# Decoder layer on one core: the four output-weight splits of a head group placed one by one in the order of VectorE and ScalarE

## The reference, cut to what matters

```
x = layernorm(x + attention(x))            # 4 x 512 tokens, width 512
x = layernorm(x + scan_block(ctx, z=x))    # a state-space scan, 16 states
x = layernorm(x + experts(x))              # shared and 16 routed experts

# attention, differential: 8 heads in 4 groups g, each with two maps
p = softmax(q1 k1) - lam * softmax(q2 k2)  # causal
o = p v;  o = o * rsqrt(mean(o*o) + eps) * subln_w * (1 - lambda_init)
return o.reshape(B, S, 2048) @ out_w.T + out_b

# scan, in 512 channels and 16 states
state = state * exp(dt * A) + (dt * u) * b;  y = sum over states of state * c
```

## Time and profile before

| | us |
|---|---|
| median of 3 runs (lowest, highest) | 1616.1 (1615.11, 1616.11) |
| the profiled execution | 1615.29 |
| its span, first to last instruction | 1613.4 |
| busy: TensorE, VectorE, GpSimd, ScalarE | 1397.1, 1294.5, 1137.9, 1045.1 |
| mean granted TensorE clock | 0.933 of full speed |

### The profile page before, as it was taken

One profiled execution on the slowest core, in us unless ns is written; L12 is line 12 of the kernel. 1 busy time (PEld: TensorE's weight loads), 2 busy tenths in 40 slices (PEclk: granted clock), 3 DMA queues, 4 the chain that ended last, 5 costly groups with the idle time before them and its releaser, 6 DMA issues.

```text
span 1613.4 us, 23141 instructions
## 1 busy us (share of the span) xinstructions
PE 1397.1 (87%) x7536; PEld 1139.5 (71%) x7536; DVE 1294.5 (80%) x2377; ACT 1045.1 (65%) x2411; POOL 1137.9 (71%) x613
## 2 busy tenths in 40 slices
PE   3655789999999989899989899986579998998996
PEld 1213678877888978788878788874367676776784
DVE  4898688998888998888989899898548577486575
ACT  3888466766666767667657666664458567577474
POOL 1335489888889987789988799998576266266263
PEclk8777889999999999999999999998799999999998
DMA  5485636667856675765666765675342122112121
GB/s 166 151 292 205 187 93 172 172 153 170 215 150 138 173 178 155 210 150 126 177 189 168 188 161 123 159 188 107 113 143 79 27 94 77 59 60 65 31 68 60
DMA packets 130313, 225.50 MB, mean 140 GB/s; under 512 B 11704, under 2 KB 61376, under 8 KB 128656
## 3 DMA queue, kind: packets, MB, share of 16 engines
q1 hardware_dynamic: 120400, 188.36, 36.9%
q0 software_dynamic: 9792, 35.66, 14.2%
HBM read 145.99 MB, written 77.99 MB: 139 GB/s over the span
## 4 chain that ended last, share of the span: by engine, by line
PE 40%; DVE 23%; issue 12%; POOL 11%; ACT 8%; DMA 5%; SPq 1%; POOLq 0%; DVEq 0%; ACTq 0%
PE banks L607 10%; PE banks L609 9%; PE banks L608 9%; POOL act_buf L1976 5%; DVE negmax L1118 3%; PE banks L1522 3%; DMA x_lo<-scratch_xs 3%; PE banks L1523 2%; PE banks L1524 2%; DVE state L1178 2%; DVE prob L1132 2%; DVE banks L423 1%; DVE banks L2051 1%; DVE qT_lo L1108 1%; ACT banks L944 1%
## 5 line engine op out<-in xcount | busy, mean ns | idle before, releaser
L1311 POOL TENSOR_TENSOR state<-state,Cn 128x1024 f32<-128x1024 f32 x100 | 244.9, 2449 | 74.9 <-DVE state L1178 74.0
L1976 POOL TENSOR_TENSOR act_buf<-act_buf,wb 128x512 f32<-128x512 f32 x128 | 165.5, 1294 | 172.3 <-ACT act_buf L1882 170.2
L1286 POOL TENSOR_TENSOR state<-dtu_sb,Bn 128x1024 f32<-128x1024 f32 x103 | 249.1, 2419 | 27.3 <-DMA Bn<-scratch_bc 25.5
L1178 DVE TENSOR_TENSOR_SCAN state<-banks,state 128x512 f32<-128x512 f32 x206 | 249.8, 1213 | 2.6 <-ACT banks L998 1.8
L998 ACT ACTIVATE banks<-dt_sb,negA 128x512 f32<-128x512 f32 x256 | 177.1, 692 | 91.0 <-DVE state L1178 72.7
L607 PE MATMUL banks<-x_hi,w_hi 128*128 128x512 f32 (+1 forms) x512 | 190.1, 371 | 47.1 <-DVE qT_lo L1108 13.3
L609 PE MATMUL banks<-x_hi,w_lo 128*128 128x512 f32 (+1 forms) x512 | 180.8, 353 | 0.0
L608 PE MATMUL banks<-x_lo,w_hi 128*128 128x512 f32 (+1 forms) x512 | 180.3, 352 | 0.0
L607 PEld LDWEIGHTS banks<-x_hi,w_hi 128*128 128x128 f32 x512 | 103.0, 201 | 68.6 <-issue 27.8
L2051 DVE TENSOR_TENSOR banks<-banks,act_buf 128x512 f32<-128x512 f32 x136 | 94.3, 694 | 49.9 <-POOL act_buf L1976 26.1
L2041 DVE TENSOR_TENSOR hid_lo<-banks,hid_hi 128x512 fp32r<-128x512 f32 x136 | 93.7, 689 | 46.2 <-ACT hid_hi L1894 44.3
(11 more groups left out here) (226 smaller groups left out, 4592.8 us busy)
## 6 DMA issues: line engine op xcount, KB each, us to landing
scratch_y<-state POOLq DMA_DIRECT2D x52, 512.0 KB, 5.9
x_hi<-scratch_xs SPq DMA_DIRECT2D x32, 512.0 KB, 5.8
x_lo<-scratch_xs SPq DMA_DIRECT2D x32, 512.0 KB, 9.2
Cn<-scratch_bc SPq DMA_DIRECT2D x64, 256.0 KB, 3.8
Bn<-scratch_bc SPq DMA_DIRECT2D x64, 256.0 KB, 4.1
scratch_acc<-acc_sb SPq DMA_DIRECT2D x64, 256.0 KB, 2.1
wb<-scratch_wT SPq DMA_DIRECT2D x64, 256.0 KB, 3.3
acc_sb<-scratch_acc SPq DMA_DIRECT2D x48, 256.0 KB, 3.1
```

The source lines that it names most:

```text
L1178: nc.vector.tensor_tensor_scan(row, dA[:, :], row, 0.0, ALU.mult, ALU.add) \
L1286: nc.gpsimd.tensor_tensor(ring(k), dtu[:, 2 * h:2 * h + 2, :], Bn[:, state % NB, :].unsqueeze(1).broadcast_to([P, 2, T]), ALU.mult).then_i ...
L1311: nc.gpsimd.tensor_tensor(to, ring(k), Cn[:, state % NB, :].unsqueeze(1).broadcast_to([P, 2, T]), ALU.mult).then_inc(S["gated"], 1)
L1976: nc.gpsimd.tensor_tensor(act_[:, N % 3, :], act_[:, N % 3, :], wb[:, E % 3, :], ALU.mult) \
```

## The change

In turn 16g+1 split 9 moves from right behind split 8 to the end of the turn, behind the scan and the low part of the projection; on ScalarE the high part of piece 9 moves behind the high part of the projection. In turn 16g+2 split 11 moves behind a scan and a row maximum; on ScalarE its high part moves behind the squares of the heads. The instructions themselves are the same, and so are those of TensorE, GpSimd and SyncE.

```diff
@@ scalar(), turn p @@
             if p % 16 == 2 and p < NM:
                 stage_high(NSTAGE * (p // 16) + 10)
-                stage_high(NSTAGE * (p // 16) + 11)
             if 1 <= p <= NM:
                 squares(p - 1)
+            if p % 16 == 2 and p < NM:
+                stage_high(NSTAGE * (p // 16) + 11)
...
             if p % 16 == 1 and p < NM:
                 stage_high(NSTAGE * (p // 16) + 8)
-                stage_high(NSTAGE * (p // 16) + 9)
             if 2 * p + 1 + AHEAD < NPROJ:
                 proj_high(2 * p + 1 + AHEAD)
             if 2 * p + 1 in W_AT:
                 stage_high(W_AT[2 * p + 1])
+            if p % 16 == 1 and p < NM:
+                stage_high(NSTAGE * (p // 16) + 9)
@@ vector(), turn p @@
             if p % 16 == 2 and p < NM:
                 stage_low(NSTAGE * (p // 16) + 10)
-                stage_low(NSTAGE * (p // 16) + 11)
             if p < NM:
                 scan(4 * p + 1)
                 row_max(2 * p + 1)
+            if p % 16 == 2 and p < NM:
+                stage_low(NSTAGE * (p // 16) + 11)
...
             if p % 16 == 1 and p < NM:
                 stage_low(NSTAGE * (p // 16) + 8)
-                stage_low(NSTAGE * (p // 16) + 9)
             if p < NM:
                 scan(4 * p + 3)
             if 2 * p + 1 + AHEAD < NPROJ:
                 proj_low(2 * p + 1 + AHEAD)
             if 2 * p + 1 in W_AT:
                 stage_low(W_AT[2 * p + 1])
+            if p % 16 == 1 and p < NM:
+                stage_low(NSTAGE * (p // 16) + 9)
```

## The result

The changed kernel takes 1639.0 us (median of 4 runs, 1633.3 to 1643.9) beside 1615.6 (1611.4 to 1616.1): a ratio of 1.0149, interval [1.0117, 1.0181]. Timed again on another occasion it took 1635.5 us (1635.1 to 1635.9, 4 runs), ratio 1.0134 [1.0114, 1.0153]. The prediction was 1636, slower. The execution that was profiled took 1633.3 us (span 1631.4); against the profiled one of before (span 1613.4) that is 18.0 us, and the traces are compared on these two.

What follows compares the result with a forecast made beforehand. TensorE was taken to set the pace between the changed places; 11.3 us of later `project_out` plus 9.1 us of clock, 20.4, on 1615.3 gave 1636. Range 1621 to 1645 for eight in ten.

Steps and rivals of the forecast that it cites:

- Step 3: VectorE behind held split 9: `negmax` 1.71 us late, yet `qT_lo` of turn 18 0.35 early in group two, 0.66 elsewhere.
- Step 8: Clock falls behind new idle time before `project_out`: 1.6 us once, 2.5 three times, 9.1; turn 17's possible 1.7 uncounted.
- S: Start of `qT_lo` in turn 18, from which split 11's end (S + 5.57) and `project_out` (S + 5.64) were forecast.
- The rule that the prediction took from two places: A VectorE split that comes while a GpSimd multiplication runs stands still until its end, then needs 0.54 us.
- step 4: Turn 17: ScalarE's part costs nothing; piece 11's load, issued later, lands at 451.9 with 1.8 us of cover.
- the top of the range: Upper end of the forecast's own range, 1643: stalls and clock up to 4 x (3.42 + 3.4) = 27 us.
- second case: Split 11 held before `project_out`, but the clock stays up: 1625 us, chance 0.09.
- The other cases: Split 11 not held, 1618 us (0.07); neither split held, faster, 1610.5 (0.04); something else, such as turns 19 on changing (0.04).

Runs made afterwards that it cites:

- e1: Kernel before with only the move of split 9 in turn 16g+1; splits 10 and 11 stay a pair: 1614.5 us, ratio 0.9996.
- e3: Changed kernel, with GpSimd's gating waiting for split 9 in turn 16g+1 and split 11 in turn 16g+2: 1621.3 us, ratio 1.0049 to the kernel before.
- e5: Changed kernel with 14 more matmuls per group on TensorE before the output projection's wait for split 11: 1624.9 us, ratio 1.0069 to the kernel before.
- e4: Kernel before, with GpSimd's drive (L1286) in turn 16g+1 waiting for splits 8 and 9: 1606.5 us, ratio 0.9943; again 1602.7 us, 0.9938.

## Why the prediction was right

*Turn 17.* Right in each step, counted from the start of split 8: the scan at +2.51 (forecast 2.52), `qT_lo` at +3.64 (3.65), GpSimd's L1311 at +3.79 (3.81), split 9 done at +6.71 (6.73), `negmax` at +6.64 (6.67). TensorE's wait fell by 0.66 us as said in three groups; in the first it fell by 0.26, with the projection 0.65 us earlier all the same.

*The start of turn 18.* The forecast put `qT_lo` at +10.10 in the second group; it came at +10.01, 0.44 us early instead of 0.35. In the other three groups it came at 9.92, 10.01 and 10.01, where it had been at 11.24, 11.32 and 11.32: 1.3 us early, not 0.66. This is the term that was off most. Step 3 took TensorE's 0.66 us as the limit there, with the slow projection left as it was; in this trace that projection took 4.40 to 4.45 us in all groups, and in none the 5.29 of three groups before, so that VectorE, with the late `hT_lo`, was the limit everywhere. Step 8 had named this as a possible 1.7 us and counted none. The stalls came to 9.3 us instead of 11.3. The trace of the second timing of the changed kernel shows the other side: in its third group the projection took 5.29 us again, VectorE waited for ScalarE's `qT_hi`, split 11 waited 0.41 us for its high part, and `project_out` came at +16.32 instead of +15.68. Its stalls come to 9.9 us. So part of this term is chance. It has a floor, too: with 14 matmuls added, the projection ran at full speed in two groups and `project_out` came at +15.62 all the same.

*Turn 18.* Split 11 took 2.74 us, ended at S + 5.52 (forecast 5.57), `project_out` at S + 5.66 (5.64). The kernel with the second half alone and the one in which GpSimd waits show that it is split 11, and that GpSimd lengthens it. The rule that the prediction took from two places holds wherever it can be read: in the twelve traces every split of 128x512 that starts during a GpSimd multiplication and has a row of its own, over 200 rows, ends 0.53 to 0.56 us behind that one's end. The load of piece 11 had the cover that step 4 gave it: in the first trace VectorE goes from `negmax` to split 11 without a wait in all four groups.

*The clock.* Forecast 9.1 us (1.6 once and 2.5 three times), measured 7.8 (2.45, 1.35, 1.58 and 2.45) on the output projections and some 0.6 more on the first matmuls behind them (226.17 to 229.20 and 949.36 to 952.61 us for twelve matmuls, 3.03 and 3.25 instead of 2.83). The second trace gives 8.0. A small part was a misreading: the projection of the fourth group ends at 924.96, not at 925.1 or later, so it took 5.29 us and not 5.4, and the 2.5 should have been 2.4. And the top of the range, 4 x (3.42 + 3.4), uses 3.4 us for the clock where step 8 had 3 as the bound. The kernel with 14 matmuls in each of the new idle times confirms it as a separate term: its ratio lies 0.8 percentage points, 13 us, below the first series of the changed kernel and 0.65, 10.5 us, below the second. The forecast's second case (held, clock up) said 1625, and that kernel took 1624.9, which is luck: the clock still fell in two groups of its trace.

*The sum.* 20.4 us forecast; 18.0 between the two profiled executions, 23.4 and 20.5 between the medians of the two series. The executions of the changed kernel differ by up to 11 us, and their mean clock with them: 0.930 at 1633.3 us, 0.924 at 1643.9. A mean lower by 0.006 is 0.006 x 1640 / 0.5 = 20 us more at the lower level, in which a busy TensorE loses half, 10 us. So the spread fits the clock. That the stalls are alike in every execution is likely by the two traces (9.3 and 9.9 us), and not shown for the others. The mechanism and both terms were right, each a little too large; that the two medians lie on either side of 1636, by 3.0 and 0.5 us, is in part the luck of which executions were timed.

The other cases fell: GpSimd did not come later than VectorE through `negmax` (it led by 0.15 us, 459.62 to 459.77, exactly the margin named), and the turns from 19 on kept their length.

## What to carry to other kernels

Before moving a VectorE instruction that, like these splits, reads two operands from SBUF, look at what GpSimd does at the new place. A multiplication that ran there held the split to its end each time, and since GpSimd was released by the scan that stands shortly in front of splits 9 and 11, it happened in all four groups of both traces of the changed kernel. A semaphore that lets the longer, less urgent GpSimd instruction start behind the short urgent one took the hold away (3.25 to 1.42 us for a pair); look then at what the later GpSimd instructions meet (here the next pair, 1.41 to 2.06 us). And a wait on TensorE can have two prices, the wait and the clock behind it; where the wait can't be removed, matmuls without use in it paid for themselves here.

## What the runs showed of the hardware that was not expected

- An idle time of 2.55 us on TensorE can be enough for the clock to fall, and need not be. Behind that of turn 17 it fell in groups 2 to 4 of both traces of the changed kernel, though the wait was 0.66 us shorter than before. In the three other kernels that have this wait (`e1`, `e3`, `e5`: 2.54 to 2.59 us) it fell in five of these nine groups, and the projection took 2.86 to 2.91 us in the other four. Behind the waits of 1.39 us (`e4`) it did not fall in any. So the length of the idle time alone does not tell the clock, and what else decides it is open.
- Even 1.76 us can be followed by it: in front of the output projection of `e3` the wait was that long in three groups, and the clock was 0.60 behind two of them and 1.00 behind the third.
- How long the projection of turn 17 runs at the lower clock differed between groups in the trace before (4.45 us in the second, 5.28 and 5.29 in the third and fourth, for the same work after the same 3.21 us of idle time), which is why a forecast from one group's row is good to a microsecond and no better.
